# Graph attention and aggregation on one core: the second pair of row tiles by seven block products

## What is computed

```python
q, k, v = x @ Wq.T + bq, key @ Wk.T + bk, value @ Wv.T + bv
s = (q @ k.T) / 64 * adj
s = where(abs(s) < 1e-5, -1e9, s)
x1 = layernorm(x + softmax(s) @ v @ Wm.T + bm)
out = layernorm(x1 + relu((adj @ x1) @ W.T + b))
```

## Time and profile before

| | us |
|---|---|
| median of 3 runs (lowest, highest) | 2017.74 (2016.58, 2018.73) |
| the profiled execution, its time | 2020.22 |
| its span, first to last instruction | 2018.5 |
| TensorE (PE) busy | 1999.5 (99%), 9243 matmuls |
| VectorE (DVE) busy | 1460.6 (72%) |
| ScalarE (ACT) busy | 685.8 (34%) |

### The profile page before, as it was taken

How to read it: one execution, slowest core, us unless ns; L and a number is a source line. 1 busy time by engine, 2 the same in 40 slices (tenths; PEclk the granted TensorE clock), 3 DMA queues, 4 the chain that set the end, 5 groups by cost and what they waited for, 6 DMA issues and landing times.

```text
span 2018.5 us, 29096 instructions
## 1 busy us (share of the span) xinstructions
PE 1999.5 (99%) x9243; PEld 916.0 (45%) x9243; DVE 1460.6 (72%) x3370; ACT 685.8 (34%) x847; POOL 96.5 (5%) x141
## 2 busy tenths in 40 slices
PE   8999999999999999999999999999999999999998
PEld 5444444444444444444444444444444444444443
DVE  7875666656666666777777777788888668888887
ACT  5854333434444443433333333344444210000000
POOL 6000000000000000000000000000000000000000
PEclk9999999999999999999999999999999999999999
DMA  7667878677777778877666766677777995555551
GB/s 286 240 166 161 202 175 207 151 163 160 179 175 175 187 165 203 201 167 167 164 161 163 166 161 161 162 168 183 183 178 211 232 275 141 126 130 137 131 136 58
DMA packets 566263, 351.22 MB, mean 174 GB/s; under 512 B 483520, under 2 KB 487616, under 8 KB 564288
## 3 DMA queue, kind: packets, MB, share of 16 engines
q1 hardware_dynamic: 548416, 279.26, 55.1%
q0 software_dynamic: 17792, 71.31, 15.4%
HBM read 176.95 MB, written 88.60 MB: 132 GB/s over the span
## 4 chain that ended last, share of the span: by engine, by line
PE 97%; DVE 1%; SPq 1%; DMA 1%; issue 0%; ACT 0%; DVEq 0%
PE ps L950 33%; PE ps L930 33%; PE ps L1090 17%; PE ps L901 4%; PE ps L985 4%; PE ps L971 4%; PE ps L1057 2%; SPq L559 0%; DMA wd<-in_wm_t 0%; PE ps L867 0%; DMA x1T<-x1hl 0%; DVE wv_s L1477 0%; DVE wmT_s L1473 0%; DVE xT L1556 0%; SPq L538 0%
## 5 line engine op out<-in xcount | busy, mean ns | idle before, releaser
L950 PE MATMUL ps<-V,PT 128*128 128x512 f16 x3072 | 673.3, 379 | 0.3 <-issue 0.3
L930 PE MATMUL ps<-KT,thl 128*128 128x512 f16 x3072 | 673.1, 379 | 0.0
L950 PEld LDWEIGHTS ps<-V,PT 128*128 128x128 f16 x3072 | 300.4, 98 | 362.9 <-issue 1.0
L930 PEld LDWEIGHTS ps<-KT,thl 128*128 128x128 f16 x3072 | 300.6, 98 | 362.2
L1708 DVE SCALAR_TENSOR_TENSOR prob<-ps,c_now,adjh 128x512 f32<-128x512 f32 x256 | 191.8, 750 | 263.3 <-PE ps L930 262.0
L1271 ACT ACTIVATE small<-prob 128x512 f32<-128x512 f32 x256 | 161.1, 630 | 621.4 <-DVE prob L1708 336.0
L1737 DVE SCALAR_TENSOR_TENSOR Phl<-prob,Phl 128x2048 f16<-128x2048 f32 x64 | 146.7, 2291 | 74.4 <-ACT Phl L1284 74.3
L1721 DVE CUSTOM_DVE_ANT_0 prob<-prob,small 128x512 f32<-128x512 f32 x256 | 174.5, 683 | 0.0
L1276 ACT ACTIVATE prob<-prob,nbias,inv 128x2048 f32<-128x2048 f32 x64 | 134.0, 2094 | 98.6 <-DVE nbias L1730 98.6
L1714 DVE TENSOR_SCALAR small<-small,eps_s,neg_s 128x512 f32<-128x512 f32 x256 | 138.9, 542 | 20.6 <-ACT small L1271 20.6
L1284 ACT ACTIVATE Phl<-prob 128x2048 f16<-128x2048 f32 x64 | 122.3, 1910 | 7.1
(11 more groups left out here) (208 smaller groups left out, 1693.7 us busy)
## 6 DMA issues: line engine op xcount, KB each, us to landing
adjh<-in_adj POOLq DMA_DIRECT2D x64, 512.0 KB, 5.3
adj_bf<-adjh SPq DMA_DIRECT2D x64, 512.0 KB, 4.7
t_in<-t_dram SPq DMA_DIRECT2D x64, 256.0 KB, 3.5
x_in<-in_x SPq DMA_DIRECT2D x64, 256.0 KB, 4.6
xraw<-in_x_t SPq DMA_DIRECT2D x8, 1024.0 KB, 7.9
t_dram<-tq POOLq DMA_DIRECT2D x8, 1024.0 KB, 5.6
o_dram<-z_out SPq DMA_DIRECT2D x32, 256.0 KB, 2.8
o_in<-o_dram SPq DMA_DIRECT2D x32, 256.0 KB, 4.5
```

The source lines that it names most:

```text
L930: last = nc.tensor.matmul(ps[:, BS + c, :], thl[:, b, s, k * P:(k + 1) * P], KT[:, m, k, c * C:(c + 1) * C], start=(n == 0), stop=(n == 3 ...
L950: last = nc.tensor.matmul(ps[:, BU + b, :], PT[:, b, s, m, :], V[:, v, m, :], start=(m == 0 and q == 0), stop=(m == MT - 1 and q == 2))
```

## The change

PLAIN is 1 instead of 2: the second pair goes by seven products too. With that:

- TensorE: plain pair 0 accumulates in banks 2 and 3. Ahead of the last `rows_product`, 8 matmuls of pair 1 (half of product 0) take the place of 16. Behind pair 0, the seven products of pair 1 are written out, in the order 0, 1, 4, then the first 11 blocks of 2, 3, 6, 5, then, after a wait for all signed sums, the rest of those four.
- SyncE: parts 0 and 1 of AT11 go before the b1 load and x1T(31), parts 2 and 3 behind the store of x1(31).
- VectorE: the adjacency sums 0 and 1 of pair 1 stand before the wait for the last row product, the sums 3 and 2 right behind it, all ahead of the first `joined`. Pair 0's results are taken out of PSUM (`take`) after `last_sums(EARLY + 2)`, the rest of its outputs follows all signed sums. Pair 1 is put together by `pair` as the others are.
- Since product 4 is made third, the waits on the count of products are mapped for the first `pair` (`made_at`), and SyncE waits for 7 products instead of 6.

```diff
-    PLAIN = 2
+    PLAIN = 1
...
+                sp.wait_ge(ph_in[1], 16 * NT)
+                sp.wait_ge(pl_in[1], 16 * NT)
+                for part in range(2):
+                    adj_part(1, 1, part)
                 sp.wait_ge(y_st, 16 * (NT - TC))
                 sp.dma_start(b1_rep[:, :], b1.rearrange("(a n) -> a n", a=1).to_broadcast([P, D])).then_inc(s_bm, 16)
                 turn_x1(NT - 1)
                 store_x1(NT - 1, 1)
-                sp.wait_ge(ph_in[1], 16 * NT)
-                sp.wait_ge(pl_in[1], 16 * NT)
-                for part in range(PARTS):
+                for part in range(2, PARTS):
                     adj_part(1, 1, part)
...
-                            sp.wait_ge(s_prod, 7 * q + 6)
+                            sp.wait_ge(s_prod, 7 * q + (7 if q == 0 else 6))
...
-                    bank = 2 * (p % 2) + k
+                    bank = 2 + k
...
-                aggregate(1, 0, 0, 8)
+
+                pe.wait_ge(at_in[1][0], 16 * PARTS)
+                product(0, adj_block(1, 0, 0), upper(0), 0, NP // 2)
                 rows_product(NT - 1)
...
-                aggregate(1, 0, 8, NT)
-                aggregate(1, 1, 0, NT)
...
+                product(0, adj_block(1, 0, 0), upper(0), NP // 2, NP)
+                product(1, adj_block(1, 0, 1), lower(0))
+                pe.wait_ge(s_comb, 3)
+                pe.wait_ge(u_mg, NT)
+                product(4, adj_sum(3), lower(1))
+                for c in range(3):
+                    pe.wait_ge(ts_ld[c], 16)
+
+                pe.wait_ge(f_out, 1)
+                product(2, adj_sum(0), signed(0), 0, EARLY)
+                pe.wait_ge(f_out, 2)
+                product(3, adj_sum(1), signed(1), 0, EARLY)
+                pe.wait_ge(s_comb, 4)
+                pe.wait_ge(s_z, NT)
+                product(6, adj_sum(2), signed(2), 0, EARLY)
+                pe.wait_ge(at_in[1][1], 16 * PARTS)
+                product(5, adj_block(1, 1, 1), signed(3), 0, EARLY)
+                pe.wait_ge(t_lo2, NP)
+                product(2, adj_sum(0), signed(0), EARLY, NP)
+                product(3, adj_sum(1), signed(1), EARLY, NP)
+                product(6, adj_sum(2), signed(2), EARLY, NP)
+                product(5, adj_block(1, 1, 1), signed(3), EARLY, NP)
...
+                for b in range(2):
+                    dve.wait_ge(ab_st[b], 16 * NT)
+                for i in range(2):
+                    adj_sum(i, None, PLAIN % 2, PLAIN // 2)
+
+                dve.wait_ge(y_mm, NT)
+                for i in (3, 2):
+                    adj_sum(i, None, PLAIN % 2, PLAIN // 2)
+                joined(EARLY)
+                last_sums(EARLY)
+                joined(EARLY + 1)
+                last_sums(EARLY + 1)
+                last_y_low(NT - 1)
...
+                joined(EARLY + 2)
+                signed_low(EARLY)
+                last_sums(EARLY + 2)
+                dve.wait_ge(s_bm, 32)
+                for k in range(2):
+                    dve.wait_ge(f_mm, k + 1)
+                    take(k, ps[:, 2 + k, :], 0)
+                for m in range(EARLY + 3, NP):
+                    joined(m)
+                    signed_low(m - 2)
+                    last_sums(m)
+                signed_low(NP - 2)
+                signed_low(NP - 1)
+                for k in range(2):
+                    output(k, k, 0)
+                    result(k, k)
```

More of the change, by code:

```diff
@@ L1043, in _, with product, upper, lower @@
                         project(g - 2, b, NT // 2 + i - 1)
+                def product(bank, left, right, m0=0, m1=NP):
+                    for m in range(m0, m1):
+                        last = nc.tensor.matmul(ps[:, bank, :].rearrange("p (s d) -> p s d", s=2), left(m), right(m),
+                                                start=(m == 0), stop=(m == NP - 1))
+                    if m1 == NP:
+                        last.then_inc(s_prod, 1)
+                def upper(h):
+                    return lambda m: Y[:, m, :, h * H:(h + 1) * H]
+                def lower(h):
+                    return lambda m: Y[:, NP + m, :, h * H:(h + 1) * H]
+                def signed(i):
+                    return lambda m: (Ta, Tb)[m // PT2][:, m % PT2, i, :, :]
+                def adj_block(h, k, half):
+                    return lambda m: AT[h][k][:, NP * half + m, :]
+                def adj_sum(i):
+                    return lambda m: (S12, S34)[i // 2][:, i % 2, m * P:(m + 1) * P]
                 def aggregate(p, k, m0, m1):
-                    bank = 2 * (p % 2) + k
+                    bank = 2 + k
                     if m0 == 0:
@@ L1109, in seven @@
                 def seven(q, h, turn):
                     def read(step):
[L1112 to L1118, removed]
+                        pe.wait_ge(c_step, 11 * (q - 1) + step)
                     pe.wait_ge(at_in[h][0], 16 * (turn + PARTS))
-                    if not isinstance(q, int) or q > 0:
-                        pe.wait_ge(s_cp, q)
@@ L1123, in seven @@
-                    plain_out(0)
+                    pe.wait_ge(s_cp, q)
                     product(0, adj_block(h, 0, 0), upper(0))
                     read(1)
-                    plain_out(1)
                     product(1, adj_block(h, 0, 1), lower(0))
                     pe.wait_ge(s_comb, 4 * q + 1)
[L1129 to L1132, removed]
@@ L1148, in seven @@
                     product(4, adj_sum(3), lower(1))
-                for p in range(PLAIN, PLAIN + 2):
+                for p in range(PLAIN + 1, 4):
                     seven(p - PLAIN, p % 2, p // 2)
@@ L2087, in _, with take @@
                 last_y_low(NT - 1)
[L2088 to L2095, removed]
+                def take(k, src, stored):
                     wait(dve, out_st[k], 16 * stored)
@@ L2183, in pair @@
                     dve.wait_ge(c_step, 11 * q + 9)
-                    output(u, 1, cs[:, 1, :], q + PLAIN)
+                    take(1, cs[:, 1, :], q + PLAIN)
+                    output(u, 1, q + PLAIN)
                     if nxt:
@@ L2195, in pair @@
                     result(u + 1, 0)
-                for p in range(PLAIN, PLAIN + 2):
+                for p in range(PLAIN, 4):
                     pair(p - PLAIN, p % 2, p // 2, ((p + 1) % 2, (p + 1) // 2))
```

63 lines of the change are left out of this document (23 added, 40 removed).

## The result

The changed kernel takes **2025.97 us** in the median of 6 runs (2023.76 to 2029.38), the kernel before 2017.45 beside it; the ratio is **1.0043 [1.0033, 1.0053]**. That is slower by 8.5 us, outside my range (2016.8 to 2025.5) and beyond my forecast of 2022.9. The direction and the stop that I named are there; the amount is not. One execution of the kernel before beside f1 to f3 took 2637.49 us at a granted clock of 0.75; the medians leave it out.

The account below looks back on a forecast made before the run. TensorE was taken to bound the kernel (busy 99%). Stop net of the saved matmuls +2.7, pushed transfers +0.8 and clock +1.7 gave +5.2 us on 2017.74, so 2022.9 us; range 2016.8 to 2025.5.

Parts of the forecast that it names:

- The stop at the low part: TensorE idles 5.1 us for Y 31's low part, queued on VectorE behind AT11 and four sums; net +2.7 us.
- The pushed transfers, d: AT11's parts 0 and 1, moved ahead on SyncE, push Y loads, x1T and what follows by 0.8 us; bounds 0 and 2.0.
- The chain's end, 1650.9 + d: Time when the low part of Y 31 is ready on VectorE, after AT11, four sums and 7.98 us more.
- What is late next on VectorE: After the low part, VectorE's extra work, block sums instead of plain outputs, costs nothing as long as its cover holds.
- the 1.6 us of cover: Block sums for the next pair's third product are done at E + 5.3; TensorE comes at E + 6.9.
- The rival of the caught part: Part 3 of AT11, caught by the Ta load, lands some 15 us later: about 2038 us; chance 0.12.
- The clock: After the stop TensorE's clock falls to the 1.2 GHz level, costing 1.7 us; bounds 0 and 1.7.
- The other side: AT11 in by 1635.4 means no change, by 1633.9 a gain of 1.6 us; chance 0.22 in all.
- The slower side: The whole kernel comes out slower by over 0.2%; chance 0.58.

Follow-up runs that it names:

- f1: Changed kernel, Y loads of quarters 2 and 3 held until all of AT11 has landed, 15 matmuls of product 1 moved ahead as cover: 2020.63 us, ratio 1.0008.
- f2: As f1 without the covering matmuls (changed kernel with the Y loads held until all of AT11 has landed): 2024.34 us, ratio 1.003.
- f3: Kernel before, AT11 parts 0 and 1 ahead of b1, Y loads held until all of AT11 landed, a plain aggregation as cover: 2020.27 us, ratio 1.0013.
- e1: Changed kernel with the four adjacency sums behind the low part of Y's last tile on VectorE: 2023.25 us, ratio 1.0022.
- e2: Changed kernel with 23 matmuls of products 0 and 1 ahead of the last block row's aggregation on TensorE: 2023.63 us, ratio 1.0027.
- e3: Changed kernel with 20 useless matmuls ahead of the last block row's, in TensorE's stop: 2025.35 us, ratio 1.0033.
- e4: Kernel before with only SyncE's order changed, parts 0 and 1 of AT11 ahead of b1 and x1T(31): 2023.91 us, ratio 1.0024.
- e6: Changed kernel with the Y loads of quarters 2 and 3 held until parts 0 and 1 of AT11 have landed: 2052.39 us, ratio 1.0149.
- e5: e4 with the Y loads of quarters 2 and 3 held until parts 0 and 1 of AT11 have landed: 2022.28 us, ratio 1.0033.
- e7: e1 with the Y loads of quarters 2 and 3 held until parts 0 and 1 of AT11 have landed: 2029.26 us, ratio 1.0069.
- f4: f1 with parts 2 and 3 of AT11 also moved ahead of b1 and the last row's turn: 2016.11 us, ratio 0.9996.
- e8: e1 with all four parts of AT11 in their old place, behind the last row's turn on SyncE: 2027.42 us, ratio 1.0045.

## Why the prediction was wrong

- **The stop at the low part: right.** I had 5.1 us, it was 5.09, on the engine and the line I named. AT11 and x1T(31), which set its two ends, came late by the same 2.2 us, so its length did not depend on d, as the working has it. The chain's end, 1650.9 + d, is 1653.2 on the clock of before, so with d = 2.2 it is right to 0.1 us. e1 shows that the sums' place made it.
- **What is late next on VectorE: right.** No wait in the pairs behind E; the 1.6 us of cover held. With the sums moved (e1) it does not quite: 0.73 us on a block sum.
- **The pushed transfers, d: the step that failed.** I took 0.8 us, from the engines' free share, with 2.0 as the bound. It was 2.2 in the profile, beyond the bound. The free time could bound what is hidden, not what is pushed: the parts' own 2.9 us can be pushed in full. And b1's load, which I let fall behind the parts as harmless, took engine time from the Y loads in its turn. In this trace that is the whole of it: the Y loads ended 2.35 us later, counted from rows_product(30), and x1T(31) landed right behind them. It can be far more: the same order of SyncE gave x1T(31) waits of 3.7, 7.6, 5.8 and 7.4 us in e1 to e4. There part 1 itself took 10.7 to 14.1 us, and e4's 50 GB/s at a share above 100% is no queueing of known work.
- **The rival of the caught part** (0.12) had the right mechanism at the wrong place. I looked for it at part 3 and the Ta load; in the profile of the changed kernel both part 1 (4.9 us) and part 3 (5.6 us) got through; in e1 to e4 it was part 1 that was caught, by the Y loads. The range left this rival out. The Trainium skill (DMA: Bandwidth & Descriptors, Queues, rings and completion order) has each DMA engine take turns between queues by packet; e4 goes further than that sentence, since there the large loads slowed as well (1 MB in 14.2 and 16.7 us, with 6.0 and 8.3 in the kernel before).
- **The clock: right that it falls, mis-sized.** 1.7 us forecast, with 1.7 as upper bound, 2.6 measured (changed kernel against e3). I had read one fall and taken its cost for the most there is.
- **The other side: wrong.** "The tile is in time" (0.22) asked for AT11 by 1635.4; VectorE had it at 1640.3 on that clock.

The slower side had 0.58 of the chance, which the result bears out; the two mis-sized terms, 1.4 and 0.9 us, are all of the distance from +5.2 to +7.7 but 0.2. The median lies 0.8 us further out, at +8.5, and no trace accounts for that.

What stays open: why turning transfers and large loads crawl in some meetings and not in others. The kernel before has parts of AT11 in flight with the Ta load for 18 us and moves 435 GB/s from 1640 to 1650; e6 has the same kinds of transfer in flight and moves 38 to 39 from 1656 to 1664. The traces do sort by when a part is issued. Each part of AT11 issued at least 0.9 us ahead of the next large load, with none in flight or the last about to land, was in after 4.0 to 5.7 us (part 1 of the changed kernel 0.9 us ahead: 4.9). Part 1 of e1 to e4, issued between 0.24 us ahead of the first Y load and 0.28 behind it, took 10.7 to 14.1. Parts issued behind the Ta load, or in e5 to e7 behind the Y loads, took 18 to 48, as they landed only about when the large loads did. No run varied that distance alone, and it does not explain why e6 was so much slower than e7. Nor do I have traces of the other executions of e4 and e5, whose times spread over 15 and 25 us; that the collision falls differently in them is inferred.

## What to carry to other kernels

Before moving a transfer ahead in one queue, list what the other queues will have in flight at its new time; a free share of the DMA engines is no bound on the delay. When a move must be made, move the whole dependent set and make the large loads wait for it (f4), rather than half of it (e5 to e7 only moved the collision). A wait that is added to an in-order engine takes the whole risk of its source with it: in e6 the sums stood ahead of the last low part, and a tile that was in at 1679.7 stopped TensorE for 40.7 us.

## What was not expected of the hardware

- Turning transfers of 256 KB, alone, land in 4 to 6 us. Meeting loads of 1 MB or more they took from 5 to 48 us, and the loads themselves from 6 to 43; in the worst stretches (e2, e4, e6) 38 to 91 GB/s were moved at shares of 0.7 to 1.7.
- TensorE's clock did not answer to the length of a stop alone. Stops of up to 1.34 us cost nothing, and neither did 2.26 and 3.37 us in e7 and the 3.10 us ahead of rows_product(31) in the changed kernel. 2.18 (e7), 2.20 (f3) and 3.69 us (e1) cost 1.7 us each, 5.34 (e6) 1.4, 5.84 (e3) 1.5, 6.85 (e8) 1.8 and 40.69 (e6) 2.0. 3.76 (f1), 5.09 (changed), 6.79 (f2), 7.44 (e4) and 7.60 us (e2) cost 2.6 to 2.7. So the price of a stop of two microseconds or more lay between nothing and 2.7 us.
